# Four layers on one core: the last layer's weight staging buffers moved in memory, all engine sequences and the dummy products written anew

## The reference

```
x = x + attention0(layernorm(x), context)   # 16 heads, causal, bf16, with biases
x = x + ffn0(layernorm(x))                  # shared part and 8 experts, routed
x = x + attention1(layernorm(x), context)   # 16 heads, f32, additive mask
x = x + switch(layernorm(x))                # 8 heads x 8 experts
```

```
xv  = einsum('bsd,hedp->bshep', x, v_w);  v = einsum('bshep,bshe->bhsp', xv, gate_v)
att = softmax(einsum('bhqp,bhkp->bhqk', q, k) * SCALE)
ctx = einsum('bhqk,bhkp->bqhp', att, v)
out = einsum('bshep,hepd->bsd', ctx[:, :, :, None, :] * gate_o[..., None], o_w)
```

## Time and profile before

| | us |
|---|---|
| runs of the kernel before, median (lowest to highest) | 1420.89 (1417.83 to 1421.06) |
| the profiled execution, its own time | 1420.77 |
| its span in the trace | 1419.0 |
| TensorE busy (matmul) | 1368.7, 96% |
| VectorE busy | 1275.1, 90% |
| ScalarE busy | 1223.2, 86% |
| GpSimd busy | 928.4, 65% |

### The profile page before, as it was taken

One profiled execution on the slowest core, in us unless ns is written; L12 is line 12 of the kernel. 1 busy time (PEld: TensorE's weight loads), 2 busy tenths in 40 slices (PEclk: granted clock), 3 DMA queues, 4 the chain that ended last, 5 costly groups with the idle time before them and its releaser, 6 DMA issues.

```text
span 1419.0 us, 34434 instructions
## 1 busy us (share of the span) xinstructions
PE 1368.7 (96%) x9536; PEld 922.6 (65%) x9692; DVE 1275.1 (90%) x5266; ACT 1223.2 (86%) x4234; POOL 928.4 (65%) x1409
## 2 busy tenths in 40 slices
PE   6678999999999999999999999999999999999997
PEld 3346666666676666667666666766666676666664
DVE  4678999999999999999999999999999999999986
ACT  4568888899988889998888999888999988889886
POOL 3124666667667666766766776676667667766777
PEclk9999999999999999999999999999999999999999
DMA  6421001000010100001010000101000011100000
GB/s 168 125 82 27 28 28 32 26 20 19 26 30 27 30 26 19 20 27 30 28 29 26 21 19 27 30 27 30 26 19 21 27 29 28 30 22 10 19 3 5
DMA packets 99967, 44.98 MB, mean 32 GB/s; under 512 B 21248, under 2 KB 99776, under 8 KB 99776
## 3 DMA queue, kind: packets, MB, share of 16 engines
q1 hardware_dynamic: 82080, 34.03, 8.6%
q10 hardware_dynamic: 17696, 8.75, 2.2%
HBM read 25.70 MB, written 8.52 MB: 24 GB/s over the span
## 4 chain that ended last, share of the span: by engine, by line
PE 88%; DVE 3%; POOL 3%; issue 2%; ACT 1%; SPq 1%; DMA 1%; ACTq 0%; POOLq 0%; DVEq 0%
PE psC L328 59%; PE psA L328 13%; PE psB L328 7%; PE psB L556 4%; PE psC L638 2%; SPq L3842 1%; PE psA L490 1%; POOL TE L3443 1%; POOL accO L3455 1%; DVE PTB L2409 1%; PE psB L577 1%; DVE TE L2542 1%; PE psA L443 1%; POOL v_sb L3448 0%; DMA k_rows<-Kc 0%
## 5 line engine op out<-in xcount | busy, mean ns | idle before, releaser
L1372 ACT ACTIVATE TE<-psC,gateO 128x128 f32<-128x128 f32 x1024 | 292.8, 375 | 45.1 <-PE psC L328 39.3
L1372 ACT ACTIVATE TE<-psC,gate 128x128 f32<-128x128 f32 x1024 | 294.1, 380 | 11.2 <-PE psC L328 6.7
L2542 DVE SCALAR_TENSOR_TENSOR TE<-psC,gateO,TE 128x128 f32<-128x128 f32 x1024 | 284.9, 343 | 16.4 <-PE psC L328 12.4
L2542 DVE SCALAR_TENSOR_TENSOR TE<-psC,gate,TE 128x128 f32<-128x128 f32 x1024 | 286.6, 342 | 11.1 <-PE psC L328 7.6
L3455 POOL TENSOR_TENSOR accO<-accO,TE 128x512 f32<-128x512 f32 x192 | 246.8, 1285 | 59.9 <-DVE TE L2542 47.7
L328 PE MATMUL psC<-Oh,ch 128*128 128x512 f32 x512 | 272.8, 533 | 0.0
L328 PE MATMUL psC<-Vh,xTh 128*128 128x512 f32 x512 | 262.7, 513 | 1.2 <-ACT PS L1372 0.9
L3443 POOL TENSOR_TENSOR TE<-TE 128x256 f32<-128x256 f32 x256 | 191.3, 747 | 43.5 <-DVE TE L2542 38.3
L328 PE MATMUL psC<-Vh,xTl 128*128 128x512 f32 x512 | 201.8, 394 | 0.0
L328 PE MATMUL psC<-Oh,cl 128*128 128x512 f32 x512 | 201.4, 393 | 0.0
L328 PE MATMUL psC<-Ol,cb 128*128 128x512 bf16 x479 | 186.6, 389 | 0.0
(11 more groups left out here) (233 smaller groups left out, 3437.9 us busy)
## 6 DMA issues: line engine op xcount, KB each, us to landing
bdB<-k_rows SPq DMA_DIRECT2D x128, 64.0 KB, 2.3
k_rows<-Kc SPq DMA_DIRECT2D x96, 64.0 KB, 2.0
Qs<-Qc SPq DMA_DIRECT2D x96, 64.0 KB, 1.9
raw<-in_L_ffn_v_w ACTq DMA_DIRECT2D x8, 512.0 KB, 4.1
raw<-in_L_ffn_o_w ACTq DMA_DIRECT2D x8, 512.0 KB, 3.7
x_sb<-in_x SPq DMA_DIRECT2D x32, 64.0 KB, 2.1
ctx_sb<-in_ctx SPq DMA_DIRECT2D x32, 64.0 KB, 2.0
bias_sb<-in_mask_Bx1xSxS_ff SPq DMA_DIRECT2D x32, 64.0 KB, 1.9
```

What stands on the lines that cost most here:

```text
L1372: return A.activation(o, i, func, **kw)
L2542: m = V.scalar_tensor_tensor(TE[:, i, e], psC[:, p, e * P:(e + 1) * P], gates[:, e:e + 1], TE[:, i, e], ALU.mult, ALU.add)
```

## The change

Three things change together.

1. `raw` becomes two buffers. The first, `raw0`, takes the memory of `v_sb` (the values) and later `cl`; the second, `raw1`, the memory of `TE` (the gated results). The wait for the sixteen cuts moves on ScalarE from `c_products` to the first `values`. The GpSimd step that writes `v_sb` and the VectorE steps come behind that one by their own semaphores.
2. The lists of all five engines are written anew. Every step occurs as often as before; only the order differs, in `start`, `period` and `end`.
3. The dummy products are placed anew: 107 before, 143 after, all in `start`.

```
-        with nc.sbuf_tensor("raw", [P, 2, 1024], F32) as raw:
-            pass
...
-        with nc.sbuf_tensor("PTC", [P, H1, P], F32) as PTC, nc.sbuf_tensor("v_sb", [P, H1, P], F32) as v_sb:
-            pass
+        with nc.sbuf_tensor("PTC", [P, H1, P], F32) as PTC:
+            with nc.sbuf_tensor("raw0", [P, H1 * P], F32) as raw0:
+                pass
+            with nc.sbuf_tensor("v_sb", [P, H1, P], F32) as v_sb:
+                pass
...
+        with nc.sbuf_tensor("raw1", [P, H1 * P], F32) as raw1:
+            pass
+        raw = (raw0, raw1)
         TE = sb("TE", [P, RING, HALF, P])
...
# ScalarE, c_products
                 act.wait_ge(c_y, 2 * b + i + 1)
-                act.wait_ge(s_lo, 4 * H1)
                 act.wait_ge(c_s, 2 * b)
...
# ScalarE, values
                 act.wait_ge(c_gate, 3 * b + 3)
+                if n == 0:
+                    act.wait_ge(s_lo, 4 * H1)
...
# VectorE, start: where the second layer of sequence 0 begins
                 a_stats2(0, 2)
+                a_norm2(0)
                 cut(3)
+                cut(4)
                 a_stats(2, 0)
                 a_stats(2, 1)
-                a_norm2(0)
-                cut(4)
-                a_stats(2, 2)
                 a_top(0, 0)
...
# GpSimd, start
-                more_constants()
+                a_causal(0, 0)
+                a_causal(0, 1)
                 a_root(1)
-                zeros()
-                a_causal(0, 0)
-                a_masks(1)
-                a_causal(0, 1)
                 a_causal(0, 2)
                 a_causal(0, 3)
+                a_masks(1)
+                more_constants()
+                zeros()
+                a_root2(0)
                 a_keys(1)
                 a_values(1)
                 a_queries(1)
-                a_root2(0)
...
# TensorE, start: sequence 1 ahead of the third layer of sequence 0
                 a_xt(1)
-                warm(3)
+                warm(8)
                 a_values(1)
                 a_queries(1)
+                warm(1)
+                a_x1t(0)
                 warm(13)
-                a_x1t(0)
-                warm(6)
                 a_route(0)
...
                 a_scores2(1, 0)
                 a_scores2(1, 1)
+                warm(3)
+                a_scores2(1, 2)
+                a_scores2(1, 3)
                 b_trans(0, 1)
-                a_scores2(1, 2)
                 b_trans(0, 2)
+                warm(1)
+                a_pvs(1)
+                warm(2)
                 b_trans(0, 3)
+                a_ut(1)
                 b_pvs(0)
-                a_scores2(1, 3)
...
# TensorE, period (the old list's first and last steps of the part)
+                b_trans(i - 2, 3)
+                a_scores2(i - 1, 0)
                 a_scores2(i - 1, 1)
-                b_trans(i - 2, 3)
+                c_scores(i - 3, 0)
                 values(i - 4, 1, 0)
-                c_scores(i - 3, 0)
...
                 c_logits(i - 2)
-                c_trans(i - 3, 1)
                 values(i - 3, 0, 1)
                 b_scores(i - 1, 3)
+                c_trans(i - 3, 1)
...
                 values(i - 3, 1, 1)
-                a_scores2(i, 0)
...
# ScalarE, period
                 b_exp(i - 1, 0)
-                c_trans(i - 3, 1)
                 c_gexp(i - 2)
+                b_exp(i - 1, 1)
                 values(i - 3, 0)
-                b_exp(i - 1, 1)
                 b_trans(i - 1, 0)
                 b_exp(i - 1, 2)
                 c_products(i - 2, 0)
                 c_products(i - 2, 1)
+                c_trans(i - 3, 1)
                 b_exp(i - 1, 3)
...
# ScalarE, start
                 a_x1t(0)
-                a_values2(1)
+                cut(5)
                 a_gap(0)
-                cut(5)
...
# SyncE, start
-                masks(0)
-                bias(0)
-                inputs(1)
                 a_keys(0)
+                masks(1)
                 a_masks(0)
                 weights_ffn()
-                masks(1)
-                no_keys()
+                inputs(1)
+                masks(2)
                 b_keys(0, 0)
                 a_masks(1)
-                masks(2)
+                no_keys()
+                inputs(2)
                 b_keys(0, 1)
-                inputs(2)
                 a_keys(1)
```

More of the change, by code:

```diff
@@ L877, in start @@
                 b_keys(3)
-                values(0, 6, 1)
                 values(0, 6, 0)
+                a_queries(4)
                 b_proj(2)
-                a_queries(4)
                 values(0, 7, 1)
@@ L1003, in start @@
                 c_products(3)
+                b_trans(4, 1)
                 values(2, 0, 0)
-                b_trans(4, 1)
+                values(2, 1, 1)
                 b_trans(4, 2)
-                values(2, 1, 1)
                 a_maxt(5)
@@ L1038, in start @@
                 values(2, 6, 1)
+                a_queries(6)
                 values(2, 6, 0)
+                values(2, 7, 1)
+                values(2, 7, 0)
                 b_keys(5)
-                values(2, 7, 1)
-                a_queries(6)
-                values(2, 7, 0)
                 outputs(2, 0, 1)
@@ L2562, in start @@
             def start():
+                ones()
+                operand_q()
+                hidden_keys()
                 a_stats(0, 0)
@@ L2584, in start @@
                 a_withmax(0)
+                selectors()
                 cut(0)
+                a_stats(1, 0)
+                a_stats(1, 1)
+                a_stats(1, 2)
                 cut(1)
-                b_keys(0)
+                a_norm(1)
                 a_attend(0, 0)
@@ L2645, in start @@
                 a_stats2(1, 2)
-                c_stats(0, 1)
-                c_stats(0, 2)
+                cut(13)
                 a_norm2(1)
-                cut(13)
+                c_stats(0, 0)
+                a_stats(3, 0)
+                b_keys(1)
                 a_top(1, 0)
@@ L3511, in start @@
                 a_causal(2, 2)
+                b_below(1, 2)
+                b_below(1, 3)
                 a_causal(2, 3)
+                a_masks(3)
                 a_keys(3)
@@ L4018, in start @@
                 b_keys(2, 1)
+                masks(4)
+                b_queries(2)
+                masks(5)
                 bias(3)
-                b_queries(2)
+                inputs(5)
                 a_keys(4)
+                a_masks(4)
                 a_queries(4)
-                a_masks(4)
                 b_keys(3, 0)
                 b_keys(3, 1)
-                bias(4)
                 b_queries(3)
-                inputs(5)
-                masks(5)
+                store(0)
                 inputs(6)
```

1038 lines of the change are left out of this document (516 added, 522 removed).

## The result

| | before | after |
|---|---|---|
| median of the runs (lowest to highest), us | 1420.89 (1417.83 to 1421.06) | 1433.55 (1432.53 to 1434.96) |
| ratio to before, 95% interval | | 1.0100 (1.0089 to 1.0111) |
| span of the profiled execution, us | 1419.0 | 1431.2 |

One of five executions of the kernel before took 3207.93 us, which no other came near, and is left out of the comparison.

What follows compares the result with a forecast made beforehand. It took TensorE's work and short waits to bound the middle, with an earlier filling moving everything one for one. Its terms, -5.1 - 1.5 - 2.2 = -8.8 us on 1420.8, gave 1412.0 us, 8-in-10 range 1403.5 to 1421.5.

Steps and rivals of the forecast that it cites:

- third term: Period, 25 times: four b_trans transposes cover TensorE's 0.18 us wait for Q2; -2.2 us, bounds 0 and -4.5.
- What bounds the kernel: Middle: only TensorE's work and short waits count, 41.4 us a layer; about 95 us are filling and draining.
- First term: Start, sequence 0: a_norm2(0) and a_root2(0) earlier bring x2 at 44.1 instead of 49.21 us; -5.1 us.
- Second term: Start, sequence 1: a_scores2(1, 2) and (1, 3) ahead of b_trans(0, 1) to (0, 3) and b_pvs(0); -1.5 us.
- Memory: ScalarE's wait for all cuts leaves c_products; 0 us for the memory itself, at most 1.6 us gained.
- Dummies: Start: the 36 more lie in TensorE's idle gaps before the middle and cost nothing; without that cover 7.8 us.
- The slower rival: Period: TensorE's values(·, 1, 1) waits 0.55 us for the bank of ScalarE's c_trans(·, 1) copy; 1425.8 us, chance 0.15.

Runs made afterwards that it cites:

- e2: Changed kernel with one added wait: GpSimd's outputs(b,7) waits until VectorE has finished a_maxt(b+4); no instruction moved. 1410.19 us, ratio 0.9935.
- e3: Kernel before with two neighbouring GpSimd instructions exchanged in the period: outputs(i-7,7) ahead of a_masks(i-2). 1442.08 us, ratio 1.0159.
- e4: Changed kernel with one TensorE step of the period put back: c_trans(i-3,1) ahead of values(i-3,0,1). 1455.23 us, ratio 1.0254.
- e12: Changed kernel with GpSimd's outputs(b,7) alone moved between b_below(·,2) and b_below(·,3); result(b,0) left behind a_masks. 1420.58 us, ratio 1.0012.
- e7: Kernel before with one TensorE move in the period: b_trans(i-1,3) ahead of a_scores2(i,0). 1426.41 us, ratio 1.0051.
- e5: Kernel before with one VectorE move in start: a_norm2(0) ahead of a_stats(2,0) and a_stats(2,1). 1419.5 us, ratio 1.0000.
- e11: Kernel before, three moves in start: a_norm2(0) before a_stats(2,0); a_stats(2,0) to (2,2) behind a_second(0); GpSimd's a_root2(0) earlier. 1416.6 us, ratio 0.9979.
- e6: Kernel before with the memory edit alone: raw split into raw0 and raw1, no instruction moved. 1421.12 us, ratio 1.0011.
- e8: Changed kernel with the added GpSimd wait for a_maxt(b+4), and all 143 dummy products left out. 1416.93 us, ratio 0.9985.
- e1: Changed kernel with GpSimd's outputs(b,7) and result(b,0) moved between b_below(·,2) and b_below(·,3), into a gap. 1410.1 us, ratio 0.9934.

## Why the prediction was wrong

*What failed* is the third term, the period. It priced one gap of TensorE, the wait for Q2, and took every instruction of the period to last as long as before. What VectorE and GpSimd might cost each other was put at nothing, in one sentence: "By that rule one more cut beside b_below would add 0.85 us to the sum; I can't place it and leave it out." The rule was read in the filling, where it costs once, and never asked of the period, where the change sets five lists anew and each meeting counts 24 times. The missing term is the hold at MtA: 1.34 - 0.23 = 1.11 us on VectorE, of which TensorE feels 0.86 (its wait) to 1.0 (42.21 - 41.19, the period). Against e2, which differs by one wait alone, it is 1433.55 - 1410.19 = 23.4 us.

The sum without it, 1412.0, is 1.8 us from what e2 measured, and part of that is luck. From the rows of MtA and the spans, e2 against the kernel before gains 7.1 us up to 330 us (6.6 were forecast) and 4.8 in 23 periods (2.0 forecast), and loses 1.3 behind them, where nothing was forecast.

The Trainium skill, "SBUF — State Buffer", section "Who interferes with whom", says that a VectorE instruction with two SBUF inputs contends with a GpSimd instruction that reads SBUF, that casts can take part when their operands meet conditions, and, of VectorE's modes with two ports, that whoever issues first gets the pair of ports that they share for the whole instruction while the other fully blocks. The rows of e3, e4 and e12 look like such a full block, of the subtraction as well as of the cast, and the held instruction ends within 0.1 us of the addition. One row does not fit: a_masks' tensor_scalar reads SBUF too, and MtA beside it took 0.23 us before and 0.36 at most. The runs show the hold; that the ports are its cause is the skill's account.

*What bounds the kernel* was right: a tenth of a microsecond in the period counts 2.5 us in the end, in e3, e7 and e12 as well. The trace of before showed TensorE without a single wait there, so the question to ask of each engine was by how little. The margin was 0.11 us, between an instruction of VectorE and one of GpSimd that share no data and no semaphore.

*The trace of before showed the hold already*, at a place where nobody waited. An addition of VectorE with both inputs in SBUF begins within an addition of GpSimd (719.56 to 720.34) and ends 0.08 us behind it:

```profile
719.56 0.78 POOL L3443 TENSOR_TENSOR TE<-TE 128x256 f32<-128x256 f32 x1
720.05 0.37 DVE L2324 TENSOR_TENSOR ob<-obA,bob 128x128 bf16<-128x128 bf16 x1
```

In the changed kernel it begins at the end of one instruction of GpSimd, 0.05 us ahead of the next, and takes half of that:

```profile
721.41 0.18 DVE L2337 TENSOR_TENSOR ob<-obA,bob 128x128 bf16<-128x128 bf16 x1
```

*First term* (-5.1): right in the changed kernel. This is VectorE there; xTA is at 38.28 us on ScalarE, and the granted clock from 38.61 to 43.85 was 1.00:

```profile
32.41 0.35 DVE L2277 TENSOR_SCALAR xnA<-x,mvA,rsA 128x128 f32<-128x128 f32 x1 [0.68 <-POOL rsA L3358]
36.83 0.29 DVE L2270 BATCH_NORM_STATS2 stA<-x_sb 128x6 f32<-128x128 f32 x1
43.85 0.29 DVE L2386 TENSOR_TENSOR x<-psA,x 128x128 f32<-128x128 f32 x1 [1.39 <-PE psA L332]
```

xnA was forecast at 32 to 33, x2 at 44.1. But the one move that the term was told by is worth nothing alone (e5). With the root earlier on GpSimd and the routing ahead of the wait for sequence 2's input, it gave 2.6 us in the kernel before (e11); in the changed kernel that input comes without a wait (the row at 36.83).

*Second term* (-1.5): a_scores2(1, 3) was forecast 5 to 8 us earlier than 69.62 and runs in a group of eight products from 61.27, some 8 us earlier. With the first term the start gives 7.4 us at the first row of the middle, where 6.6 were forecast. The second term wasn't run alone.

*Third term* (-2.2, bounds 0 and -4.5): with the lock gone the period is 41.19 instead of 41.40, 0.21 x 25 = 5.3 us, a little above the good bound. As a single move it has the other sign (e7), so which of the period's moves gave the gain isn't shown.

*Memory* (0): right (e6). *Dummies* (0 for the 36 more): not run apart; all 143 together give 6.7 us (e8), so that a cost of 7.8 for the new ones is unlikely.

*The slower rival*, a new wait in each period of 0.55 us, had the kind and nearly the size, but the wrong place: TensorE never waited for PTC in the changed kernel. Its mechanism is real, as e4 shows at 1.0 us, though at the product before. A period of 41.6 or more had been named as the sign of a wrong prediction, and it is 42.2.

## What to carry to other kernels

In a saturated loop, lay VectorE's and GpSimd's lists beside each other: for each short VectorE instruction with its inputs in SBUF that somebody waits for, write down by how much it misses the next long GpSimd instruction. A margin of 0.1 us is not a margin, and a new order anywhere can use it up. The sign in a trace is an instruction whose duration, not whose waiting time, has grown, or which takes longer than the same one elsewhere; the cure, in e2 and e1, is to let the long one wait for the short one, or to move it into a gap. And a stall that ends in a list of many steps is rarely cured by moving one of them.

## What the runs showed of the hardware

A 128 x 16 cast with one input in SBUF is held just as the subtraction with two: 1.08 us in e3 and 1.34 in e4 instead of 0.22. GpSimd's one-input instruction on 16 partitions held neither for its 0.64 us, but it is not free: beside it MtA took 0.23 us before and up to 0.36 in e3, and the cast 0.22 before and 0.30 in the changed kernel. Of the transfers of queries, which take 1.9 us, the longest in each trace took 3.8 to 4.7; in e5, one wait of TensorE at such a transfer, 1.78 us, was about what the move had gained.
